# Who makes the high parts of the probability sums, and who adds the single key's row: a cross-attention kernel on one core

## The reference

```python
def sdpa(q, k, v):
    scale = 1.0 / jnp.sqrt(jnp.asarray(D, q.dtype))
    scores = jnp.einsum('bshd,blhd->bhsl', q, k) * scale
    attn = jax.nn.softmax(scores, axis=-1)
    return jnp.einsum('bhsl,blhd->bshd', attn, v)

out_txt = sdpa(q, k_txt, v_txt)      # 1243 keys
out_img = sdpa(q, k_img, v_img)      # 257 keys
x = x + ((out_txt + out_img).reshape(B, S, INNER) @ o_w + o_b)
```

## Time and profile before

| | us |
|---|---|
| median of 3 runs (lowest, highest) | 1924.05 (1923.73, 1924.66) |
| profiled execution: its time / its span | 1923.51 / 1921.7 |
| PE busy | 1757.4 (91%) |
| DVE busy | 1400.8 (73%) |
| ACT busy | 985.4 (51%) |
| POOL busy | 1147.9 (60%) |

### The profile page before, as it was taken

One profiled execution on the slowest core, in us unless ns is written; L12 is line 12 of the kernel. 1 busy time (PEld: TensorE's weight loads), 2 busy tenths in 40 slices (PEclk: granted clock), 3 DMA queues, 4 the chain that ended last, 5 costly groups with the idle time before them and its releaser, 6 DMA issues. The chain is left out here.

```text
span 1921.7 us, 30704 instructions
## 1 busy us (share of the span) xinstructions
PE 1757.4 (91%) x8735; PEld 1537.2 (80%) x8735; DVE 1400.8 (73%) x2586; ACT 985.4 (51%) x1659; POOL 1147.9 (60%) x987
## 2 busy tenths in 40 slices
PE   7899979999999999999999999999992998699998
PEld 6566669888888888888898898888892887588887
DVE  4344477977978878878878879788772565577777
ACT  3354445555655655655555556556552553244443
POOL 1000178888788788788888887887862331133333
PEclk8999989999999999999999999999996999699999
DMA  3365564465554665554554565556535782133332
GB/s 109 106 214 205 193 174 111 110 120 117 122 121 112 129 128 117 122 131 115 115 134 108 115 127 125 116 115 130 101 89 187 249 275 86 64 117 108 121 108 80
DMA packets 417360, 251.19 MB, mean 131 GB/s; under 512 B 350267, under 2 KB 368827, under 8 KB 415516
## 3 DMA queue, kind: packets, MB, share of 16 engines
q1 hardware_dynamic: 417308, 250.55, 50.9%
HBM read 187.71 MB, written 60.10 MB: 129 GB/s over the span
## 5 line engine op out<-in xcount | busy, mean ns | idle before, releaser
L1322 ACT ACTIVATE p_high<-psum,key_rms 128x448 fp32r<-128x448 f32 x384 | 244.9, 638 | 396.9 <-PE psum L1145 396.8
L1143 PE MATMUL psum<-p_high,c_high 128*128 128x448 f32 (+1 forms) x768 | 287.9, 375 | 47.8 <-DVE p_low L1405 47.8
L1405 DVE TENSOR_TENSOR p_low<-psum,p_high 128x448 fp32r<-128x448 f32 x384 | 236.4, 616 | 99.8 <-ACT psum L1324 98.6
L1143 PE MATMUL psum<-u_high,c_high 128*128 128x448 f32 x768 | 286.0, 372 | 20.3 <-DVE psum L1416 14.0
L1144 PE MATMUL psum<-u_low,c_high 128*128 128x448 f32 x768 | 282.8, 368 | 0.0
L1145 PE MATMUL psum<-u_high,c_low 128*128 128x448 f32 x768 | 281.8, 367 | 0.0
L1145 PE MATMUL psum<-p_high,c_low 128*128 128x448 f32 (+1 forms) x768 | 281.4, 366 | 0.0
L1144 PE MATMUL psum<-p_low,c_high 128*128 128x448 f32 (+1 forms) x768 | 281.0, 366 | 0.0
L1416 DVE COPY psum<-beta_wide 128x448 f32<-128x448 f32 x416 | 259.4, 627 | 20.5 <-DMA beta_wide<-absorbed_biases 4.7
L1617 POOL TENSOR_TENSOR c_low<-stage,c_high 128x512 fp32r<-128x512 f32 x208 | 274.0, 1317 | 0.0
L1324 ACT ACTIVATE psum<-psum,key_rms 128x448 f32<-128x448 f32 x384 | 232.5, 606 | 0.0
(11 more groups left out here) (246 smaller groups left out, 4026.8 us busy)
## 6 DMA issues: line engine op xcount, KB each, us to landing
stage<-in_ctx SPq DMA_DIRECT2D x210, 256.0 KB, 2.8
averages<-o_raw SPq DMA_DIRECT2D x64, 448.0 KB, 5.2
o_stage<-averages SPq DMA_DIRECT2D x32, 896.0 KB, 5.6
u_raw<-absorbed_queries SPq DMA_DIRECT2D x60, 448.0 KB, 5.6
absorbed_queries<-u_stage SPq DMA_DIRECT2D x14, 1792.0 KB, 6.8
beta_wide<-absorbed_biases SPq DMA_DIRECT2D x32, 448.0 KB, 5.0
recip_wide<-reciprocals SPq DMA_DIRECT2D x32, 448.0 KB, 4.0
p_wide<-probs_by_expert SPq DMA_DIRECT2D x32, 448.0 KB, 3.6
```

Source lines behind the costliest of these rows:

```text
L1143: nc.tensor.matmul(out, high, rhigh, start=start, stop=False, **kw)
L1322: nc.scalar.activation(p_high[:, probs_slot(u), :], src, ACT.Exp, scale=key_rms[:, t:t + 1])
L1405: return nc.vector.tensor_tensor(out, a, b, ALU.subtract)
```

## The change

Three things move in the attention stage.

1. The copy that makes `p_sum_high` goes from VectorE's `split_sum` to ScalarE (`high_sum`), behind the exponentials of steps 1 and 2 (text) and of steps 7 and 8 (image).
2. What is left of `split_sum` on VectorE, the `p_sum_low`, moves one step later: to the end of steps 2 and 3 (text) and of steps 8 and 9 (image).
3. The single key's row is no longer added on VectorE; GpSimd adds it (`add_lone`), at the end of steps 5 and 6. ScalarE's `high_sum` for image waits for it (`lone_added`). `ADDS` and `added(u)` count the additions of VectorE without those of the two lone units.

```diff
-        TEXT_SUM_SPLIT, TEXT_SUMS, TEXT_RECIP = (1, 2), (3, 5), 10
-        IMAGE_SUM_SPLIT, IMAGE_SUMS, IMAGE_RECIP = (7, 8), (9, 11), 16
+        TEXT_SUM_HIGH, IMAGE_SUM_HIGH = (1, 2), (7, 8)
+        LONE_ADDED = (5, 6)
+        TEXT_SUM_SPLIT, TEXT_SUMS, TEXT_RECIP = (2, 3), (3, 5), 10
+        IMAGE_SUM_SPLIT, IMAGE_SUMS, IMAGE_RECIP = (8, 9), (9, 11), 16
...
+            def high_sum(it, s, half):
+                n = 4 * it + 2 * s + half
+                last = 2 * (LONE if s == 0 else TILES) - 2 + half
+                act.wait_ge(sum_added, ADDS * it + added(last) + CREDIT["sum_added"])
+                if s == 0:
+                    act.wait_ge(lone_added, 2 * it + half + 1)
+                act.wait_ge(sum_wide, n - 1 + CREDIT["sum_wide"])
+                copy(p_sum_high[:, half, :], p_sum[:, 2 * s + half, :]).then_inc(sum_high_ready, 1)
...
+                    if has_prev and step in TEXT_SUM_HIGH:
+                        high_sum(it - 1, TEXT, TEXT_SUM_HIGH.index(step))
+                    if step in IMAGE_SUM_HIGH:
+                        high_sum(it, IMAGE, IMAGE_SUM_HIGH.index(step))
...
             def add(it, u):
+                if t == LONE:
+                    return
...
             def split_sum(it, s, half):
-                dve.wait_ge(sum_added, UNITS * it + last + 1 + CREDIT["sum_added"])
                 dve.wait_ge(sum_wide, n - 1 + CREDIT["sum_wide"])
-                nc.vector.tensor_copy(p_sum_high[:, half, :], p_sum[:, 2 * s + half, :]).then_inc(sum_high_ready, 1)
                 dve.wait_ge(sum_high_ready, n + 1)
...
+            def add_lone(it, half):
+                gp.wait_ge(exp_done, UNITS * it + 2 * LONE + half + 1 + CREDIT["exp_done"])
+                gp.wait_ge(sum_added, ADDS * it + added(2 * LONE - 2 + half) + CREDIT["sum_added"])
+                total = p_sum[0:1, half, :]
+                nc.gpsimd.tensor_tensor(total, lone_probs[0:1, half, :], total, ALU.add).then_inc(lone_added, 1)
...
+                    if step in LONE_ADDED:
+                        add_lone(it, LONE_ADDED.index(step))
```

More of the change, by code:

```diff
@@ L50 @@
 AVERAGES = UNITS - 2
+ADDS = AVERAGES
 TOK = 112
@@ L98, in averaged, with added @@
     return u + 1 - min(max(u + 1 - 2 * LONE, 0), 2)
+def added(u):
+    return averaged(u)
 def probs_slot(u):
@@ L911, in attend @@
         o_stored = [sem("o_image_stored"), sem("o_text_stored")]
-        lone_copied = sem("lone_copied")
+        lone_copied, lone_added = sem("lone_copied"), sem("lone_added")
         lone_step, lone_summed, lone_high_ready, lone_split = (
@@ L1377, in tail @@
                     carried(it, step)
+                    if step in TEXT_SUM_HIGH:
+                        high_sum(it - 1, TEXT, TEXT_SUM_HIGH.index(step))
                     text_sums(it, step)
@@ L1457, in add @@
                     dve.wait_ge(sum_split, 4 * (it - 1) + 2 * s + half + 1 + CREDIT["sum_split"])
-                    added = nc.vector.tensor_copy(total, part)
+                    done = nc.vector.tensor_copy(total, part)
                 else:
-                    dve.wait_ge(sum_added, UNITS * it + u - 1 + CREDIT["sum_added"])
-                    added = nc.vector.tensor_tensor(total, part, total, ALU.add)
-                added.then_inc(sum_added, 1)
+                    dve.wait_ge(sum_added, ADDS * it + added(u) - 2 + CREDIT["sum_added"])
+                    done = nc.vector.tensor_tensor(total, part, total, ALU.add)
+                done.then_inc(sum_added, 1)
             def split_sum(it, s, half):
-                last = 2 * (IMG_TILES if s == 0 else TILES) - 2 + half
                 n = 4 * it + 2 * s + half
-                dve.wait_ge(sum_added, UNITS * it + last + 1 + CREDIT["sum_added"])
                 dve.wait_ge(sum_wide, n - 1 + CREDIT["sum_wide"])
-                nc.vector.tensor_copy(p_sum_high[:, half, :], p_sum[:, 2 * s + half, :]).then_inc(sum_high_ready, 1)
                 dve.wait_ge(sum_high_ready, n + 1)
@@ L1503, in take @@
                 if u // 2 != LONE and (has_next or u + SC_RING < UNITS):
-                    dve.wait_ge(sum_added, UNITS * it + u + 1 + CREDIT["sum_added"])
+                    dve.wait_ge(sum_added, ADDS * it + added(u) + CREDIT["sum_added"])
                     seed_after(it, u, has_next)
```

## The result

| | before | changed |
|---|---|---|
| median, us (lowest, highest) | 1923.89 (1920.56, 1924.66) | 1952.74 (1951.12, 1955.92) |
| profiled execution: its time / its span | 1923.51 / 1921.7 | 1955.92 / 1954.1 |
| TensorE's wait for `p_low` / for `p_sum_low`, us | 47.8 / 1.1 | 3.4 / 75.0 |
| mean granted clock of TensorE | 0.972 | 0.956 |

The changed kernel is slower: the ratio is 1.015, with a 95% interval from 1.0138 to 1.0162, 28.8 us by the medians. The forecast was 1936.5 with a range of 1919 to 1946. The direction was right, the size was not.

The account below looks back on a forecast made before the run. It took TensorE, busy for 91% of the span with four breaks in a batch, as the bound. 1923.51 + 11.8 for batches + 0.8 at the stage's end gave 1936.1, the median 0.5 above; it said 1936.5, range 1919 to 1946.

Parts of the forecast that it names:

- 2.94 us of work: TensorE's work from the first text sum to the average of step 4, read from the profile before.
- 4.66 us of work: TensorE's work from the scores of step 8 to the first image sum, read from the profile before.
- Text 1.82 for 2.04: Steps 1 to 4: the subtraction waits for u_low, so TensorE starts the first text sum 2.04 us late.
- Image 2.94 for 2.59: Steps 7 to 10: the subtraction waits for u_raw, so TensorE starts the first image sum 2.59 us late.
- +0.74: Growth of TensorE's breaks per batch, 4.63 us for 3.89; counted for 16 batches, 11.8 us.
- GpSimd's additions: Two one-row additions of 448 columns ahead of step 7's c_twice, taken at 1.16 us each.
- The first rival: GpSimd's additions cost under 0.75 us each: 1920 to 1927 us, no measurable change; chance 0.14.
- The wait for GpSimd's instruction: VectorE's copies and subtractions wait until GpSimd's instruction ends, then take 0.25 or 0.48 us.
- The second rival: The subtraction does not wait for GpSimd; a batch is 1.14 us faster, 1906 us; chance 0.09.
- The third rival: VectorE reaches the subtractions before u_low and u_raw begin; the four breaks about halve, 1890 to 1900 us; chance 0.07.
- ScalarE's covers: Steps 1 to 4 and unit 8: exponentials up to 1.1 us later, or behind GpSimd's second addition, delay nothing.
- The end of the stage: The last text sum follows ScalarE's copy and the subtraction, starting at 1448.4 for 1447.62: +0.8 us.

Follow-up runs that it names:

- e3: Changed kernel with eight unused matmuls added on TensorE per batch, just ahead of its wait for the first image subtraction; 1928.77 us, ratio 1.0013.
- e1: Changed kernel with only VectorE's two image subtractions put back to steps 7 and 8; 1906.01 us, ratio 0.9899.
- e2: Changed kernel with all four subtractions back at steps 1, 2, 7 and 8; 1881.51 us, ratio 0.9773.
- e5: Kernel before with only the high-part copies moved to ScalarE; 1881.57 us, ratio 0.9775.
- e4: Changed kernel with the single key's row added on VectorE again; 1931.18 us, ratio 1.0041.
- e6: Kernel before with only the single key's row moved to GpSimd; 1917.88 us, ratio 0.9966.
- e7: Kernel before with only the split moved one step later, copy and subtraction together on VectorE; 2006.18 us, ratio 1.0429.
- e8: e2 with VectorE making the first text high part in place of ScalarE; 1885.72 us, ratio 0.9797.
- e12: The same kernel as e2, run again on the chip of e9, e10 and e11; 1878.86 us, ratio 0.9766.
- e9: Changed kernel with GpSimd's first u_low and first u_raw moved behind the tile's c_low and c_twice of steps 3 and 9; 1932.37 us, ratio 1.0043.
- e10: e2 with GpSimd's first u_low and first u_raw moved to steps 3 and 9; 1870.01 us, ratio 0.9712.
- e11: e10 with VectorE also making the first text high part; 1870.14 us, ratio 0.9708.

## Why the prediction was wrong

**The step that failed** is one that the text did not write down as a step: it counted every microsecond of TensorE's work at the speed of the kernel before ("2.94 us of work", "4.66 us of work", "it was at 732.00"), whatever the length of the break ahead of it. The breaks that it forecast were longer than any in the loop's batches before (1.46), and behind the longer one of each batch TensorE's clock fell to 1.2 GHz: ten spells, five of 6.8 and five of 3.4 us, in 15 batches. A spell of 3.4 us cost 1.55 us (76.4 less 74.8), one of 6.8 cost 2.7. Those add up to 21 us of profiled time, and e3, which has one spell of 3.4 us left, reaches the end of the stage 24.3 us earlier. The trace of the kernel before had the sign, in its first batch, where TensorE waits longer. Its timeline there, and three windows:

```profile
269.49 0.47 PE L1143 MATMUL psum<-p_high,c_high 128*128 128x448 f32 x1 [2.68 <-DVE p_low L1405]
```

```profile
264.00:270.50 6.50, 3.82 (x21) 3.25 (x21) 3.47 (x8) 1.68 (x3) 5.76 (x6) 1.00 1.04 321
271.00:274.20 3.20, 3.20 (x12) 2.94 (x12) 2.33 (x4) 1.58 (x3) 2.85 (x3) 0.50 0.70 286
275.00:281.00 6.00, 5.81 (x29) 4.66 (x28) 5.93 (x13) 3.22 (x6) 3.41 (x5) 1.00 0.52 130
```

A break of 2.68 us, and 1.5 us behind it the clock at half for some 3 us. Whoever forecasts a break of 2.59 us in every batch had here a row that says what may follow one. It is no rule: the same first break, of 2.67 to 2.69 us, has such a spell behind it in the traces of before, changed, e1, e2 and e5, and none in those of e3, e4, e6, e7, e8 and e12.

**The breaks: the mechanism right, two sizes off.** Text 1.82 for 2.04: the subtraction ended 3.62 us behind its norm, as worked out (3.61), TensorE started 0.25 behind that (0.03 taken), but the norm stood 2.05 us ahead of TensorE's asking (566.28) and not 1.60. Image 2.94 for 2.59. From the text sum to the norm of step 8 are 581.25-568.10 = 13.15 us, 13.18 by the forecast; but TensorE asked for the image sum 584.96-2.94-568.10 = 13.92 us behind the text sum, and not 14.25. The "work" between the breaks of before was too long: it held what a break costs beyond its row, and before there were four breaks in a batch. By the start times the matmul that ends a break comes some 0.15 us later than the bracket says, and the next one 0.1 later still (its row takes 0.46 to 0.48 us, the others 0.36): the break of 0.93 cost 1.19. Counted so, the breaks of a batch were 5.3 us before (3.89 in brackets) and are 5.7 now (4.76), and what is left, TensorE's work, is 69.1 us in both. So the term of the sum that was mis-sized is the batch: 74.8 us with full clock, **+0.4** and not +0.74. With +0.4 the sum gives 1931 without a fall of the clock, and e3 shows 1929. The two errors had opposite signs: the batch was taken too dear by about 5 us, the clock at nothing where it cost some 20, so that the forecast was 16 us short and not 21.

**GpSimd's additions**: 1.14 and 1.15 us for 1.16, so the row of one partition costs as much as 128. The first rival (cheap additions) is refuted. The Trainium skill (GPSIMD Engine Reference, Instruction dispatch) says that every core receives the identical instruction and works on its own 16 partitions. By that the trace agrees with what the prediction drew from it.

**The wait for GpSimd's instruction** held in every case, 0.48 to 0.49 us behind the end of `u_low`, `u_raw` and, in e9, `c_low`. In the traces of before, changed, e1, e2, e9 and e10 there are 252 subtractions `p_sum_low` of more than 0.75 us, and every one ends 0.48 or 0.49 us behind the end of a GpSimd instruction. The second rival is refuted. The exclusive lock of which the Trainium skill speaks (SBUF — State Buffer, Who interferes with whom) agrees with the traces.

**The third rival** (the relief arrives) named the right doubt in the wrong place. The relief does arrive, 43 us of it, when the high parts alone move (e5). The later place of the subtraction takes it away and more: it alone is the difference between e2 and the changed kernel, 71 us.

**ScalarE's covers** held, as far as the breaks go: the first `p_low` of concern (564.81) came 0.58 us behind its norm where it was 0.34, which the subtraction's wait for `u_low` hid, and the wait for `lone_added` cost no break. In e2, with the large breaks gone, ScalarE's text copies show in the 0.80 of `gram`: with one of them taken away (e8) it is 0.35.

**The end of the stage**: from the start of the last average to the last sum are 2.69 us (1472.51 to 1475.20), in two breaks of 0.98 and 0.67. Before there were 1.83 (1445.79 to 1447.62) in one of 1.06. That is 0.86 more for 0.8 forecast.

What stays open: why the clock falls in some batches behind a break of 2.1 or 2.95 us and not in others of the same length. It came for 3.4 us behind 12 of 14 breaks of 2.15, behind 8 of 14 of 2.2 to 2.4, and longer only behind 2.94 and more; in the changed kernel in a fixed rhythm of three batches. Behind the first batch the shortest break with a fall was 1.89 us, once (e3, at 1382 us), while 15 breaks of 1.56 to 1.89 in the changed kernel had none. In the first batch of e10 it fell at a break of 1.77 (at 273.62 us); in e9 and e11 it did not at breaks of the same length. It also stays open what bounds e10, and why the text break is 0.2 us shorter in e3.

## What to carry to other kernels

A copy that waits on a shared port is best moved to an engine that does not share it; moving what is left of it behind another wait of the same chain gives the gain back. When a sum of breaks says "slower by little" and one break becomes longer than all there were, price the clock too: add a case in which TensorE runs part of each round at half clock. If the wait can't be avoided, fill it (e3); whether cutting it in two would do as well was not tested. Take what lies between two breaks from the start times of matmuls and not from the brackets. Of a bundle of edits run each part alone before the bundle is judged: here one was worth -2.3%, one -0.3% and one +4.3%.

## What the runs showed of the hardware

- Spells of half clock in the attention stage come as 3.4 or 6.8 us. Behind the first batch they began from 1.3 us before to 1.5 us after the end of a break of 2.0 us or more (once 1.89). The count: 14 breaks of 2.03 to 2.07 in e4, 4 spells of 3.4; 14 of 2.15 to 2.17 in e9, 12 of 3.4; 14 of 2.21 to 2.37 in e1, 8 of 3.4; 14 of 2.94 to 2.99 in the changed kernel, 5 of 6.8 and 4 of 3.4. The last batch has a break of 2.00 in e9 and in the changed kernel, each with a spell of 3.4. In e7, with breaks of 2.9 to 3.4 twice in a batch, there are 20.
- Eight useless matmuls in a break made a kernel 24 us faster (e3), although the work itself was not needed.
- A VectorE subtraction of 128x448 that meets a GpSimd instruction ends 0.48 to 0.49 us behind it; alone it takes 0.63.
- A one-row addition of 448 columns takes GpSimd 1.14 us (mean of 32), a 128-row subtraction of 448 columns 1.16.
